# Other byte offsets for the tiles that TensorE reads in the expert stage, and another bank order in every second expert

## The reference, cut to what matters

```
h = gelu(einsum('td,edf->etf', x, W1) + b1[:, None, :])     # 8 experts, 256 -> 1024
eo = einsum('etf,efd->etd', h, W2) + b2[:, None, :]          # 1024 -> 256
out = einsum('te,etd->td', w, eo)
```

## Time before, and how its profile is read

| | |
|---|---|
| median of 3 runs | 1735.08 us (1733.52 to 1735.17) |
| span of the profiled execution, first to last instruction | 1731.8 us |
| busy in it: PE, DVE, ACT, POOL | 1717.2, 1212.7, 1013.0, 1010.7 us |
| granted TensorE clock, mean | 0.999 |

### The profile page before, as it was taken

One profiled execution on the slowest core, in us unless ns is written; L12 is line 12 of the kernel. 1 busy time (PEld: TensorE's weight loads), 2 busy tenths in 40 slices (PEclk: granted clock), 3 DMA queues, 4 the chain that ended last, 5 costly groups with the idle time before them and its releaser, 6 DMA issues.

```text
span 1731.8 us, 26700 instructions
## 1 busy us (share of the span) xinstructions
PE 1717.2 (99%) x8480; PEld 1446.9 (84%) x8480; DVE 1212.7 (70%) x2284; ACT 1013.0 (58%) x1834; POOL 1010.7 (58%) x1722
## 2 busy tenths in 40 slices
PE   8999999999999999999999999999999999999998
PEld 7899998998888888888888888888888888888887
DVE  6787777777676666666666678766666666666666
ACT  3776677666665555555555566555555555555554
POOL 6654565455355665748483849374847566574842
PEclk9999999999999999999999999999999999999999
DMA  4100010002011111111011111222301021111101
GB/s 115 32 19 20 25 32 20 13 32 69 25 49 25 51 37 37 37 37 49 25 49 33 54 24 37 62 70 77 109 26 49 25 49 36 38 37 38 37 13 49
DMA packets 91835, 72.05 MB, mean 42 GB/s; under 512 B 11824, under 2 KB 89904, under 8 KB 91696
## 3 DMA queue, kind: packets, MB, share of 16 engines
q1 hardware_dynamic: 91552, 70.29, 14.4%
q10 hardware_dynamic: 144, 0.07, 0.0%
HBM read 61.82 MB, written 8.52 MB: 41 GB/s over the span
## 4 chain that ended last, share of the span: by engine, by line
PE 94%; issue 1%; DVE 1%; ACT 1%; POOL 0%; DVEq 0%; ACTq 0%; POOLq 0%
PE bank L1098 13%; PE bank L1100 13%; PE bank L1099 13%; PE bank L1054 11%; PE bank L1056 11%; PE bank L1055 11%; PE bank L978 3%; PE bank L1004 3%; PE bank L1018 2%; PE bank L966 2%; PE bank L965 2%; PE bank L967 2%; PE bank L999 1%; PE bank L1001 1%; PE bank L1000 1%
## 5 line engine op out<-in xcount | busy, mean ns | idle before, releaser
L1387 ACT ACTIVATE g_sb<-c_sb,b_cols 128x512 f32<-128x512 f32 x384 | 276.2, 719 | 397.7 <-DVE c_sb L1900 293.5
L1725 DVE TENSOR_TENSOR h_lo<-g_sb,h_hi 128x512 fp32r<-128x512 f32 x512 | 390.7, 784 | 102.8 <-ACT h_hi L1391 102.2
L1098 PE MATMUL bank<-h_hi,w_both 128*128 128x512 f32 x1024 | 398.8, 389 | 0.0
L1100 PE MATMUL bank<-h_lo,w_both 128*128 128x512 f32 x1024 | 398.7, 389 | 0.0
L1099 PE MATMUL bank<-h_hi,w_both 128*128 128x512 f32 x1024 | 398.4, 389 | 0.0
L2064 POOL TENSOR_TENSOR h2f<-h2f,y_sb 128x256 f32<-128x256 f32 x216 | 200.8, 962 | 284.8 <-DVE y_sb L1749 284.8
L1054 PE MATMUL bank<-t_hi,w_hi 128*128 128x512 f32 x896 | 352.0, 393 | 4.2 <-DVE p_u L1891 2.0
L1056 PE MATMUL bank<-t_hi,w_lo 128*128 128x512 f32 x896 | 348.9, 389 | 0.0
L1055 PE MATMUL bank<-t_lo,w_hi 128*128 128x512 f32 x896 | 348.8, 389 | 0.0
L1391 ACT ACTIVATE h_hi<-c_sb,b_cols 128x512 fp32r<-128x512 f32 x384 | 272.1, 709 | 0.0
L1100 PEld LDWEIGHTS bank<-h_lo,w_both 128*128 128x128 f32 x1024 | 192.2, 188 | 40.3
(11 more groups left out here) (206 smaller groups left out, 2967.6 us busy)
## 6 DMA issues: line engine op xcount, KB each, us to landing
w_raw<-w_dram SPq DMA_DIRECT2D x128, 256.0 KB, 2.9
g_rows<-gates_scratch SPq DMA_DIRECT2D x31, 512.0 KB, 8.4
x_sb<-x_dram SPq DMA_DIRECT2D x32, 128.0 KB, 2.5
x_scratch<-x_sb SPq DMA_DIRECT2D x32, 128.0 KB, 1.7
x_slabs<-x_scratch SPq DMA_DIRECT2D x4, 512.0 KB, 7.0
out_dram<-x_slabs SPq DMA_DIRECT2D x4, 512.0 KB, 3.6
h2f<-x_scratch SPq DMA_DIRECT2D x4, 512.0 KB, 3.8
wmod_raw<-wmod_dram SPq DMA_DIRECT2D x4, 256.0 KB, 3.7
```

What stands on the lines that cost most here:

```text
L1098: nc.tensor.matmul(o, w_hi, h_hi[:, ring, :], start=first, stop=False, skip_group_check=True)
L1100: done_ = nc.tensor.matmul(o, w_hi, h_lo[:, ring, :], start=False, stop=last, skip_group_check=True)
L1387: nc.scalar.activation(g_sb[:, m % 2, :], source, ACT.Gelu_apprx_tanh, bias=bias).then_inc(act_g, 1)
L1725: nc.vector.tensor_tensor(h_lo[:, m % RING, :], g_sb[:, m % 2, :], h_hi[:, m % RING, :].bitcast(F32), ALU.subtract).then_inc(dve_lo, 1)
```

## The change

It moves buffers and changes the order of part of the matmuls; no instruction of arithmetic is added or taken away.

- Slots 2 and 3 of the weights get skips of 384 and 480 bytes ahead of them, the second token part (`t_hi[1]`, `t_lo[1]`) one of 64 bytes. Slots 0 and 1 and the first token part stay.
- `h_hi` and `h_lo` become five buffers each, with skips between them, and the fourth of each starts 16 bytes into its buffer.
- `c_sb`, `g_rows` and `y_sb` lie elsewhere, and slots 2 and 3 begin earlier in memory, to make the room. As `y_sb` now lies where the attention's tiles were, the first eviction into it waits for the last stores of those.
- In experts 1, 3, 5 and 7 `down` goes through the two banks by turns: w_hi by h_hi into k = 0, then k = 1, then w_lo by h_hi into each, then w_hi by h_lo into each. The two hidden tiles that end a round's sum in a bank keep the old order. In experts 0, 2, 4 and 6 the order is the old one. Where the bank is new, both evictions are now waited for ahead of the six matmuls.

Start bytes modulo 512, worked out from the two layouts:

| | before | after |
|---|---|---|
| `t_hi`, `t_lo`, part 0 / part 1 | 448 / 448 | 448 / 0 |
| weight slots 0, 1, 2, 3 | 448, 448, 448, 448 | 448, 448, 0, 480 |
| `h_hi` and `h_lo`, ring 0 to 4 | 448 each | 0, 448, 480, 16, 128 |

```diff
+SLOT_SKIP = (0, 0, 96, 120)
+RING_SKIP = {"h_hi": (16, 112, 8, 8, 24), "h_lo": (96, 112, 8, 8, 24)}
+RING_MORE = (0, 0, 0, 4, 0)
+TOKENS_SKIP = 16
...
         def weight_slot():
 
             i = len(w1_hi)
+            if SLOT_SKIP[i] > 0:
+                keep(f"w_skip{i}", [P, SLOT_SKIP[i]])
...
+        def ring_slots(name):
+
+            made = []
+            for i in range(RING):
+                keep(f"{name}_skip{i}", [P, RING_SKIP[name][i]])
+                made.append(keep(f"{name}{i}", [P, RING_MORE[i] + UTOK], F32R)[:, RING_MORE[i]:RING_MORE[i] + UTOK])
+            return made
...
-        h_hi, h_lo = keep("h_hi", [P, RING, UTOK], F32R), keep("h_lo", [P, RING, UTOK], F32R)
+        h_hi, h_lo = ring_slots("h_hi"), ring_slots("h_lo")
...
+        keep("tokens_skip", [P, TOKENS_SKIP])
         token_parts(1)
-        g_rows = keep("g_rows", [P, 2 * UTOK])
         x1_slabs = keep("x1_slabs", [P, 2, 2 * UTOK])
+        y_sb = keep("y_sb", [P, 2, KD, UTOK])
...
+                def passes(slot, f, ring, u, k, first, last):
+
+                    w_hi, w_lo = (w2_both[slot][:, f, i, k * P:(k + 1) * P] for i in range(2))
+                    o = y_banks[u][k]
+                    nc.tensor.matmul(o, w_hi, h_hi[ring], start=first, stop=False, skip_group_check=True)
+                    nc.tensor.matmul(o, w_lo, h_hi[ring], start=False, stop=False, skip_group_check=True)
+                    return nc.tensor.matmul(o, w_hi, h_lo[ring], start=False, stop=last, skip_group_check=True)
...
+                        if e % 2 == 0 or last:
+                            done_ = passes(slot, f, ring, u, k, first, last)
                         if last and k == 0:
                             done_.then_inc(pe_y, 1)
+                    if e % 2 == 1 and not last:
+                        for n_pass in range(3):
+                            for k in range(KD):
+                                w = w2_both[slot][:, f, n_pass == 1, k * P:(k + 1) * P]
+                                done_ = nc.tensor.matmul(y_banks[u][k], w, h_lo[ring] if n_pass == 2 else h_hi[ring],
+                                                         start=first and n_pass == 0, stop=False, skip_group_check=True)
...
+                    if r == PAIRS and u == 0:
+                        for s in s_st:
+                            dve.wait_ge(s, TILES // 2 * 16 + 16)
```

More of the change, by code:

```diff
@@ L36 @@
 SPLIT_STEPS = 12
+SLOT_SKIP = (0, 0, 96, 120)
+RING_SKIP = {"h_hi": (16, 112, 8, 8, 24), "h_lo": (96, 112, 8, 8, 24)}
+RING_MORE = (0, 0, 0, 4, 0)
+TOKENS_SKIP = 16
+PROBS_ROWS = 8192
+KEYS_ROWS = 7680
 COLS_WIDE, GATE_WIDE = 32, 4
@@ L457, in adaln_block @@
         wqkv_raw = probs[1][:, 0, 0:KD * QKV].rearrange("p (k n) -> p k n", k=KD)
-        h_hi, h_lo = keep("h_hi", [P, RING, UTOK], F32R), keep("h_lo", [P, RING, UTOK], F32R)
+        rows_end = nc.sbuf_base + 4 * PROBS_ROWS
+        keys_end = rows_end + 4 * KEYS_ROWS
+        h_hi, h_lo = ring_slots("h_hi"), ring_slots("h_lo")
         g_sb = keep("g_sb", [P, 2, UTOK])
         p1_u3, u2 = keep("p1_u3", [P, UTOK]), keep("u2", [P, UTOK])
-        c_sb = keep("c_sb", [P, 2, UTOK])
+        rows_left = (rows_end - nc.sbuf_base) // 4
         with ExitStack() as first:
             sb = with_(first)
+            if rows_left > 0:
+                sb("rows_left0", [P, rows_left])
             wmod_raw = sb("wmod_raw", [P, KD, 6 * D])
@@ L471, in adaln_block @@
         with ExitStack() as first:
+            if rows_left > 0:
+                with_(first)("rows_left1", [P, rows_left])
             keys1 = keys_of(1, with_(first))
@@ L474, in adaln_block @@
             weight_slot()
-        y_sb = keep("y_sb", [P, 2, KD, UTOK])
-        if KEYS_MORE > 0:
-            keep("rest1", [P, KEYS_MORE])
+        c_sb = keep("c_sb", [P, 2, UTOK])
+        g_rows = keep("g_rows", [P, 2 * UTOK])
+        keep("rest1", [P, (keys_end - nc.sbuf_base) // 4])
         k_hi, k_lo, v_sb, v_hi, v_lo = zip(keys0, keys1)
@@ L1390, in hidden @@
                         act.wait_ge(pe_down, used(before // 4, MADE[before % 4]) + 1)
-                    nc.scalar.activation(h_hi[:, m % RING, :], source, ACT.Gelu_apprx_tanh, bias=bias).then_inc(act_hi, 1)
+                    nc.scalar.activation(h_hi[m % RING], source, ACT.Gelu_apprx_tanh, bias=bias).then_inc(act_hi, 1)
                 def cast_tokens(n):
@@ L1724, in low @@
                     dve.wait_ge(act_hi, m + 1)
-                    nc.vector.tensor_tensor(h_lo[:, m % RING, :], g_sb[:, m % 2, :], h_hi[:, m % RING, :].bitcast(F32),
+                    nc.vector.tensor_tensor(h_lo[m % RING], g_sb[:, m % 2, :], h_hi[m % RING].bitcast(F32),
                                             ALU.subtract).then_inc(dve_lo, 1)
```

## The result

The changed kernel took 1757.73 us (median of 4 runs, 1757.13 to 1760.04), the kernel before 1734.30 in the same comparison. The ratio is 1.0139, with a 95% interval of 1.0127 to 1.0151: slower by 23.4 us. The forecast was 1720 with a range of 1690 to 1755, so the direction is wrong and the time lies just outside the range.

What follows compares the result with a forecast made beforehand. TensorE, busy 99% of the span, was taken as the bound, through 0.2265 us between matmul starts. Offsets -15.3 us and all other terms 0 took 1,735.1 to about 1,720 us, range 1,690 to 1,755.

Steps and rivals of the forecast that it cites:

- the bank order: Down matmuls by turns in four of eight experts, 1,344 of them: 0 us, bounds 3 us either way.
- the waits at a new bank: First block into a bank waits for both evictions: 0 us, with 8 us of room each.
- the added wait: VectorE waits for the attention's stores ahead of the first eviction into `y_sb`, at about 532 us: 0 us.
- the moved buffers: `c_sb`, `g_rows`, `y_sb` moved, tiles at 16 or 32 bytes for ScalarE and VectorE: 0 us.
- the other engines' durations: VectorE's and ScalarE's durations in the expert stage should hold within a tenth.
- the price of an offset: Expert-stage matmuls whose operand pair gets another relation modulo 512: -3.7 ns on each of 4,138, -15.3 us.
- the stream that never settles: Expert-stage distance stays at 0.231: +18.6 us on changed pairs to +26 on all, 1,754 to 1,761; chance 0.22.
- eight kinds of relations: In the ring and slots, so each matmul meets another relation than the last and the distance stays at 0.231.
- nothing happens: The fp32r gap settles at 0.2265 wherever the operands start: 1,735 us; chance 0.25.
- The rule weighed: Skill page: TensorE never waits on another user of the memory; by it the offsets would sum to nothing.
- plain fp32: Its matmuls, 0.217 us apart at 256 columns and 0.109 at 128, were read as having a fixed part near zero.
- The 11 ns of excess: Fixed time an fp32r matmul carries over a plain fp32 one; the most to win, 5,760 x 11 ns = 63 us.

Runs made afterwards that it cites:

- the kernel with the ratio 1.0001: The kernel before with the banks by turns in experts 1, 3, 5, 7 and no byte moved: 1733.91 us, ratio 1.0001.
- the one with 1.0002: The changed kernel with all skips out and the old order of banks, its buffers left where the change puts them: 1734.83 us, ratio 1.0002 against the kernel before.

## Why the prediction was wrong, point by point

**Right:** that only the distance of two starts counts, and that it is read as stretch over count; that a byte offset can change it; the bank order at 0 (ratio 1.0001); the waits at a new bank, the added wait and the moved buffers at 0 (the wait at a new bank is in the kernel with the ratio 1.0001, the others are in the one with 1.0002); the other engines' durations within a tenth.

**The step that failed** is the price of an offset, "I take -3.7 ns, a third of the excess, on the changed pairs". It measured +4.5 ns (226.94 to 231.43), with the other sign, and as a mean over the whole stage, not only over the 4,138 whose relation changed. The step rested on one distance of 0.22 in the earlier trace rows and passed over the mean of the same rows, 0.231, which is where the changed kernel runs. Taken from the starts in the trace, the nine distances there are 235, 233, 236, 224, 231, 236, 228, 232 and 231 ns, and then the settled 227, 227, 226; the break before that one is followed by the very same nine. So the 0.22 was the one 224 of a fixed sequence, between a 236 and a 231, and no level at which a stream stays. In none of the 14 kernels did the mean fall below 0.2265.

**The rival that came true** is the stream that never settles. It was given 0.22, and its prices of +26 us on all pairs (1,761) and +18.6 on the changed ones (1,754) enclose the 1,757.7. The range ended at 1,755 because it left out the case in which untouched pairs are drawn in. They are: with only the third place of the ring moved, up products with unchanged operands lose too. The prediction spoke of eight kinds of relations; by the two layouts there are eleven. In the changed kernel, grouped by the relation of the earlier matmul, the mean distance is 230.2 ns for relation 0 (1,603 distances), 230.7 for +64, 232.5 for +32, 232.5 and 232.8 for -32 and -64. All are above 226.7. The prediction said that, if the relation counts, the up products on slots 0 and 1 with part 0 would keep 0.2265; they have relation 0, and their mean is 230.7 (658 distances). Experts 1, 3, 5, 7 and experts 0, 2, 4, 6 both lie at 231.4, as a bank order of no effect wants.

**The rival "nothing happens"** fell with the run of the offsets alone (ratio 1.0144). What stood for it, that slot, ring place and part make no difference, was true only because all of them differ by multiples of 512 bytes. In a trace where a parameter has one value throughout, its evenness says nothing on the parameter.

**The rule weighed:** the Trainium skill, page "SBUF — State Buffer", section "Who interferes with whom", has TensorE waiting on nobody. The runs do not contradict that another engine never blocks it, but kernels with the same arithmetic, and TensorE busy throughout both stretches, differ by 35 us (1,733.4 to 1,768.7) through start bytes, so 0 was not the sum.

**A reading to put right:** plain fp32. The kernel issues 116 of the matmuls `pT` by `v`, and the trace has 232 records of them (L1004), so a record, 0.217 us from the next, is half a matmul. It also takes nearly twice the 0.120 us of an fp32r matmul with the same 256 columns. So the agreement that the prediction reports for plain fp32 holds for a record counted as 512 columns, not as its 256. The 11 ns of excess come from a comparison of unlike records, and no run showed that any of them can be had back. (5,760 x 11 ns is 63 us, as the prediction has it at first, and not 62.)

**What explains the size.** Two effects are shown. A constant relation has its own settled distance: 226.7 ns for 0 and +256, 228.9 for +64, 233.3 for -32 and -64. And an odd tile leaves about ten more unsettled distances behind it, with a mean of 231 to 232. In the changed kernel the relation mostly changes after three or six matmuls and, after the first 27, never stays for more than 18. So the stream is nearly always in the second state: only 189 of its 5,689 distances stand in stretches of six or more at 226 and 227 ns, against 5,377 before. How much of the 4.5 ns is disturbance and how much the price of the relations themselves was not separated.

**What stays open:** why the relation matters and modulo what it repeats (0 and +256 alike would fit 256 as well as 512; +64 and -64 differ, so it is not 128), and the settled distance of the relations not tried alone, 16, 80, 128 and 192 among them. That the cause lies in how TensorE reads its two operands from the memory is argued: the start bytes were what was changed, and the settled patterns go on whatever the other engines do. No row shows the reads themselves. Matmuls of fewer columns and kernels with idle TensorE were not tried.

## What to carry to other kernels

When TensorE has no idle time, divide a quiet stretch by its count of matmuls; a change of one ns there is worth more than any wait off the path. Give all stationary and moving tiles of a dense fp32r stream one relation of start bytes, 0 modulo 512 being a fast one here, and look at the layout again when a small buffer is put between two large ones. Read the mean of an irregular sequence and not its best member.

## What the runs showed of the hardware that was not expected

- fp32r matmuls of 512 columns at the granted clock of 1.00 (2.4 GHz) settle at mean distances of 226.67, 228.89 and 233.33 ns, by the relation of the start bytes. Worked out from these means, they fit whole numbers of 6.667 ns: 34 in one distance, 103 in three, 70 in two. What such a step would be, no run shows.
- With the moving tile's start 32 or 64 bytes below that of the weights, modulo 512 (relation -32 or -64), a settled matmul takes 6.7 ns more, 34 us in this kernel; 64 bytes the other way takes 2.2 ns more, 12 us; 256 bytes cost nothing.
- One ring place in five that starts 64 bytes off costs 6.6 us: its own matmuls and some ten behind it, with operands untouched, lose the settled distance.
- The unsettled stretch behind a break repeats itself to the nanosecond: the same nine distances, from 235 to 231 with one of 224, at two breaks in the kernel before.
- Operands that all start 32 bytes off a multiple of 64 run as fast as before in the two stretches (2,009 and 1,811 matmuls).
